# A four-layer transformer kernel: the opening without diagonal matrices, feed-forward subtractions moved, high-half passes sent first

## The reference, cut

```python
x = x + quant_xattn(layernorm(x), fside, ctx)   # int8-style: gate/up product, silu, down product
x = x + bit_ffn(layernorm(x), w1, w2, w3)       # ternary weights, 704 hidden
x = x + xattn(layernorm(x), ctx, mask, Wq, Wk, Wv, Wo)   # 16 heads of 128
x = x + moe_ffn(layernorm(x), router, sh_gate, sh_up, sh_down, r_gate, r_up, r_down)

def smooth_quant_linear(x, w):       # quant_xattn runs it twice
    s = sqrt(max(amax_cols(x), EPS) / max(amax_cols(w), EPS))
    xs, ws = x / s, w * s
    x_scale, w_scale = amax_rows(xs) / 127, amax_rows(ws) / 127
    return round(xs / x_scale) @ round(ws / w_scale).T * x_scale * w_scale.T
```

## Time and profile before

| | us |
| --- | --- |
| median of three runs | 431.57 (431.56 to 433.33) |
| profiled execution | 431.38 |
| its span | 429.3 |
| TensorE busy | 402.8 (94%) |
| VectorE busy | 307.4 (72%) |
| ScalarE busy | 230.3 (54%) |
| GpSimd busy | 175.1 (41%) |

### The profile page before, as it was taken

One profiled execution on the slowest core, in us unless ns is written; L12 is line 12 of the kernel. 1 busy time (PEld: TensorE's weight loads), 2 busy tenths in 40 slices (PEclk: granted clock), 3 DMA queues, 4 the chain that ended last, 5 costly groups with the idle time before them and its releaser, 6 DMA issues.

```text
span 429.3 us, 8839 instructions
## 1 busy us (share of the span) xinstructions
PE 402.8 (94%) x3185; PEld 382.6 (89%) x3185; DVE 307.4 (72%) x948; ACT 230.3 (54%) x636; POOL 175.1 (41%) x294
## 2 busy tenths in 40 slices
PE   7877979999989999999999999999999999999795
PEld 7766868999979999999999999999899999998795
DVE  5599676968865888787766879777757766654544
ACT  2678656665644446666543456656453566564231
POOL 2124665565634352525533354355342233332231
PEclk9999999999999999999999999999999999999899
DMA  7997200000000020000000100000000000000000
GB/s 252 328 352 293 76 2 0 3 2 0 2 2 0 8 71 0 2 2 3 1 14 14 52 2 2 2 1 2 2 26 2 2 0 3 2 2 0 26 0 26
DMA packets 15098, 16.89 MB, mean 39 GB/s; under 512 B 1552, under 2 KB 14032, under 8 KB 15056
## 3 DMA queue, kind: packets, MB, share of 16 engines
q1 hardware_dynamic: 15056, 16.33, 11.8%
HBM read 15.28 MB, written 1.05 MB: 38 GB/s over the span
## 4 chain that ended last, share of the span: by engine, by line
PE 57%; DVE 22%; ACT 10%; issue 5%; POOL 5%; DMA 1%; DVEq 0%; POOLq 0%
PE bank_s L350 13%; PE bank_u L350 9%; PE bank_qa L350 7%; PE bank_o L350 7%; PE bank_pt L533 4%; PE bank_pt L350 4%; DVE prob L1502 3%; ACT prob L838 3%; PE bank_x L350 3%; DVE pt_lo L1513 2%; DVE ut_lo L1519 2%; PE bank_u L462 2%; ACT pt_hi L798 1%; POOL prob L1135 1%; PE bank_x L358 1%
## 5 line engine op out<-in xcount | busy, mean ns | idle before, releaser
L1135 POOL TENSOR_SCALAR prob<-prob,row_inv,valid_b 128x256 f32<-128x256 f32 x128 | 70.3, 558 | 92.6 <-DVE row_inv L1509 92.2
L838 ACT ACTIVATE prob<-prob,row_min 128x256 f32<-128x256 f32 x128 | 64.2, 502 | 68.5 <-DVE row_min L1502 68.3
L1513 DVE TENSOR_TENSOR pt_lo<-bank_pt,pt_hi 128x512 fp32r<-128x512 f32 x64 | 44.1, 688 | 18.1 <-ACT pt_hi L798 17.9
L1519 DVE TENSOR_TENSOR ut_lo<-bank_u,ut_hi 128x256 fp32r<-128x256 f32 x64 | 26.9, 421 | 35.2 <-ACT ut_hi L798 34.5
L1502 DVE CUSTOM_DVE_ANT_0 prob<-bank_s,masked 128x256 f32<-128x256 f32 x128 | 48.8, 418 | 2.9 <-PE bank_s L350 2.4
L1147 POOL TENSOR_TENSOR act_lo<-act_raw,act_hi 128x256 fp32r<-128x256 f32 x32 | 24.2, 755 | 49.2 <-ACT act_hi L903 49.2
L798 ACT ACTIVATE pt_hi<-bank_pt 128x512 fp32r<-128x512 f32 x64 | 37.6, 587 | 9.4 <-PE bank_pt L533 9.2
L350 PE MATMUL bank_o<-c_hi,ut_hi 128*128 128x256 f32 x128 | 38.7, 302 | 1.8 <-DVE ut_lo L1519 1.6
L533 PE MATMUL bank_pt<-ident,prob 128*128 128x128 f32 x256 | 38.9, 274 | 0.8 <-POOL prob L1135 0.7
L350 PE MATMUL bank_qa<-xt_hi,a_hi 128*128 128x256 f32 x126 | 39.5, 314 | 0.0
L350 PE MATMUL bank_u<-pt_hi,cx_hi 128*128 128x256 f32 x128 | 37.7, 295 | 1.6 <-DVE pt_lo L1513 1.4
(11 more groups left out here) (306 smaller groups left out, 1328.7 us busy)
## 6 DMA issues: line engine op xcount, KB each, us to landing
wq_raw<-in_wqT SPq DMA_DIRECT2D x4, 512.0 KB, 9.4
wo_raw<-in_wo SPq DMA_DIRECT2D x4, 512.0 KB, 8.9
w_raw<-in_w12T SPq DMA_DIRECT2D x2, 704.0 KB, 6.8
gate_raw<-in_gateT SPq DMA_DIRECT2D x2, 576.0 KB, 7.6
up_raw<-in_upT SPq DMA_DIRECT2D x2, 576.0 KB, 9.4
down_raw<-in_downT SPq DMA_DIRECT2D x2, 576.0 KB, 11.3
x<-in_x SPq DMA_DIRECT2D x4, 256.0 KB, 5.3
guT<-in_guT SPq DMA_DIRECT2D x4, 256.0 KB, 3.0
```

Of the source, the lines that this page charges most:

```text
L838: last = act.activation(row, row, ACT.Exp, scale=-1.0, bias=row_min[:, h % 2, t:t + 1], accum_out=row_sum[:, h % 2, t:t + 1])
L1135: last = pool.tensor_scalar(row, row, row_inv[:, h % 2, t:t + 1], valid_b[:, 0:1], ALU.mult, ALU.mult)
L1513: dve.tensor_tensor(pt_lo[:, :, :].rearrange("p s t -> p (s t)"), bank["pt"][:, :], f32(pt_hi[:, :, :].rearrange("p s t -> p (s t)")), ALU ...
L1519: dve.tensor_tensor(ut_lo[:, :], bank["u"][:, 0:T], f32(ut_hi[:, :]), ALU.subtract).then_inc(S["u_l"], 1)
```

## The change

The computation stays the same. Five things differ:

1. The diagonals are gone. A scale column, repeated 128 times along the free dimension, is itself the stationary operand and the identity moves (`q_spread`). In the opening the roots are made in two instructions and each is spread on its own; the weights' scales are spread as soon as they are there, before the rounded values are turned, and ScalarE copies them before the product.
2. The opening is ordered anew on all engines: fillers, `prep_unit`s (order 0, 2, 1, 3, other banks), ternary steps; `q_weight_scales(1)` goes from behind the ternary layer to before the second `q_dequant`; `ctx_split_lo(0)` from before the first ternary chunk to behind the second.
3. GpSimd's feed-forward subtractions: none before the ternary chunks now, two after, four after `lna`, one each in the heads 2, 4, 5, 6, 7 and 8.
4. In `bit_down`, `scores`, `mix`, `project` and `ffn_down` the passes with the high half of the newly made operand go first, behind a wait for that half alone; then comes the wait for the low half and its passes. The number of passes is the same.
5. Layer norms signal each tile by itself, and the turn waits tile by tile.

```diff
-FFN_LO_HEADS = (2, 5, 6, 8)
+FFN_HI_HEADS = (2,)
+FFN_HI_EARLY = FFN_UNITS - len(FFN_HI_HEADS)
+FFN_LO_HEADS = (2, 4, 5, 6, 7, 8)
...
+        PREP_ORDER = (0, 2, 1, 3) + tuple(range(4, 2 * PAIRS))
...
+            def turn_xn(b, kind, dst):
+
+                for t in range(NT):
+                    pe.wait_ge(S[kind + "_xn"], NT * b + t + 1)
...
             def q_spread(b, s):
-                pe.wait_ge(S["q_diag"], 2 * b + s + 1)
-                w = 512 if s == 0 else 256
-                dst = bank["x0"] if s == 0 else bank["x1"]
-                pe.matmul(dst[:, 0:w], ones[:, :], dg[:, 0:w // P, :].rearrange("p a c -> p (a c)"),
-                          start=True, stop=True).then_inc(S["q_spread"], 1)
+
+                for i in range(2):
+                    pe.wait_ge(*(S["q_root"], b + 1) if s else (S["q_roots"], q_roots_count(b, i)))
+                    columns = [root0[:, i, b, k:k + 1] for k in range(ND)] if s == 0 else [sis[:, i:i + 1]]
+                    dst, at = spread_place(b, s, i)
+                    for j, column in enumerate(columns):
+                        last = pe.matmul(dst[:, at + j * P:at + (j + 1) * P], column.to_broadcast([P, P]), ident[:, :],
+                                         start=True, stop=True)
+                    last.then_inc(S["q_spread"], 1)
+
+            def q_spread_weight_scales(b, s):
+                pe.wait_ge(S["q_scales"], 2 * b + s + 1)
+                if b > 0 and s == 0:
+                    pe.wait_ge(S["q_bf_w"], b + 1)
+                if b == 0 and s == 1:
+                    pe.wait_ge(S["prep_lo"], 4)
+                for j in (2, 3):
+                    last = pe.matmul(wscale_bank(b)[:, (j - 2) * P:(j - 1) * P],
+                                     qscale[:, s, j:j + 1].to_broadcast([P, P]), ident[:, :], start=True, stop=True)
+                last.then_inc(S["q_wspread"], 1)
 
...
-                pe.wait_ge(S["q_wdiag"], 2 * b + s + 1)
-                pe.matmul(bank["x1"][:, 0:D], ones[:, :], dg[:, 2:4, :].rearrange("p a c -> p (a c)"),
-                          start=True, stop=True).then_inc(S["q_prod"], 1)
+                last.then_inc(S["q_prod"], 1)
...
             def bit_down(b, c):
                 if c == 0:
                     pe.wait_ge(S["w3_ready"], 2)
+                    pe.wait_ge(S["prep_lo"], 8)
                 pe.wait_ge(S["bit_hi"], BIT_CHUNKS * b + c + 1)
...
-                        keep_busy(*((5, "s1"), (10, "pt"))[c - BIT_CHUNKS])
+                        keep_busy(*((3, "s1"), (4, "pt"))[c - BIT_CHUNKS])
...
             def mix(b, h):
 
-                pe.wait_ge(S["t_l"], H * b + h + 1)
+                pe.wait_ge(S["t_h"], H * b + h + 1)
                 if h >= 1:
                     pe.wait_ge(S["u_l"], H * b + h)
+                elif b > 0:
+                    pe.wait_ge(S["shared_x"], b)
                 for s in range(2):
-                    last = split_mm(bank["u"][:, 0:T], cx_hi[:, s, :], cx_lo[:, s, :], pt_hi[:, s, :],
-                                    pt_lo[:, s, :], s == 0, s == 1)
+                    for half in (cx_hi, cx_lo):
+                        pe.matmul(bank["u"][:, 0:T], half[:, s, :], pt_hi[:, s, :], start=(s == 0 and half is cx_hi),
+                                  stop=False, skip_group_check=True)
+                pe.wait_ge(S["t_l"], H * b + h + 1)
+                for s in range(2):
+                    last = pe.matmul(bank["u"][:, 0:T], cx_hi[:, s, :], pt_lo[:, s, :], start=False, stop=(s == 1),
+                                     skip_group_check=True)
                 last.then_inc(S["u_mm"], 1)
 
             def project(b, h):
...
             keep_busy(22, "pt")
             q_turn_xn(0)
-            keep_busy(24, "pt")
+            keep_busy(16, "pt")
             q_piece(0, 0)
-            keep_busy(30, "pt")
+            keep_busy(28, "pt")
+            q_spread_weight_scales(0, 0)
+            keep_busy(8, "pt")
             q_piece(1, 0)
             pe.wait_ge(S["abs_done"], 6)
             pe.matmul(bank["u"][:, 0:6], ones[:, :], gsum[:, :], start=True, stop=True).then_inc(S["gamma_mm"], 1)
             q_piece(2, 0)
             prep_unit(0)
             prep_unit(1)
+            q_piece(3, 0)
             prep_unit(2)
-            q_piece(3, 0)
             prep_unit(3)
-            keep_busy(16, "pt")
+            keep_busy(8, "pt")
             q_piece(4, 0)
+            keep_busy(18, "pt")
+            q_spread_weight_scales(0, 1)
+            keep_busy(5, "pt")
+            q_piece(5, 0)
             prep_unit(4)
+            q_piece(6, 0)
             prep_unit(5)
             prep_unit(6)
-            q_piece(5, 0)
-            q_piece(6, 0)
             prep_unit(7)
             keep_busy(24, "pt")
             bit_turn(0)
             keep_busy(6, "pt")
             pe.wait_ge(S["w12_ready"], 4)
-            pe.wait_ge(S["prep_lo"], 8)
+            pe.wait_ge(S["prep_lo"], 4)
+            pe.wait_ge(S["q_wscale"], 2)
 
             def beside_bit(c):
                 if c == 1:
@@ -812,8 +875,8 @@
...
-            def q_spread_diagonals(b, s):
...
-            def q_scale_diagonals(b, s):
-
-                pool.wait_ge(S["q_scales"], 2 * b + s + 1)
-                pool.nop(nofuse=True)
-                for j in (2, 3):
-                    last = pool.tensor_scalar(dg[:, j, :], ident[:, :], qscale[:, s, j:j + 1], 1.0, ALU.mult, ALU.mult)
-                last.then_inc(S["q_wdiag"], 1)
...
+            q_roots0()
             q_round(0, 0, 0)
-            q_scale_diagonals(0, 0)
             q_root1(0)
             q_round(0, 1, 0)
-            q_scale_diagonals(0, 1)
             power(0, "lnb")
-            pool.wait_ge(S["lnb_xn"], 1)
-            lnq_power(1, 2)
+            for c in range(BIT_CHUNKS):
+                bit_low(0, c)
+                if c == 1:
+                    lnq_power(1, 2)
             ffn_weights_lo(0)
             ffn_weights_lo(1)
-            for c in range(BIT_CHUNKS):
-                bit_low(0, c)
-            ffn_weights_lo(2)
-            ffn_weights_lo(3)
             power(0, "lna")
-            pool.wait_ge(S["lna_xn"], 1)
-            for u in range(4, FFN_LO_EARLY):
+            pool.wait_ge(S["lna_xn"], NT)
+            for u in range(2, FFN_LO_EARLY):
                 ffn_weights_lo(u)
             normalise(0, 0)
             q_roots(1)
-            q_spread_diagonals(1, 0)
             for b in range(NB - 1):
                 batch(b, False)
...
-            q_spread_diagonals0(0)
...
             ternary12_clip(1, 0)
-            prep_lo(4)
             ternary12_clip(1, 1)
-            ternary3_clip(0)
-            prep_lo(5)
-            prep_lo(6)
+            q_weight_scales(1)
             q_dequant(0, 1).then_inc(S["q_out"], 1)
             q_residual0()
             ln_stats_of(0, "lnb")
+            prep_lo(4)
+            ternary3_clip(0)
+            ln_apply(0, "lnb")
+            prep_lo(5)
             ternary3_clip(1)
-            prep_lo(7)
-            ln_apply(0, "lnb")
             dve.wait_ge(S["x_in"], 16)
             link(lnq_stats_of([1]))
+            ln_lo(0, "lnb", xt_hi, xt_lo)
+            prep_lo(6)
             lnq_variances([1])
-            ln_lo(0, "lnb", xt_hi, xt_lo)
-            ctx_split_lo(0)
             for c in range(BIT_CHUNKS):
                 bit_act(0, c)
                 if c == 0:
-                    mask_row(0)
+                    prep_lo(7)
+                elif c == 1:
+                    ctx_split_lo(0)
                 elif c == 2:
                     prep_lo(8)
                 elif c == 3:
+                    mask_row(0)
+                    dve.wait_ge(S["router_hi"], 1)
+                    dve.tensor_tensor(router_lo[:, :, :], router_raw[:, :, :], f32(router_hi[:, :, :]), ALU.subtract
+                                      ).then_inc(S["router_lo"], 1)
+                elif c == 5:
                     lnq_apply(1)
-            q_weight_scales(1)
             prep_lo(9)
             bit_residual(0)
             ln_stats_of(0, "lna")
@@ -1801,9 +1831,6 @@
             first_queries_lo(1)
             row_minima(0, 0)
             row_minima(0, 1)
-            dve.wait_ge(S["router_hi"], 1)
```

214 lines of the change are left out of this document (108 added, 106 removed).

## The result

| | before | changed |
| --- | --- | --- |
| median, us | 432.45 (431.56 to 434.01, 4 runs) | 419.16 (418.34 to 419.98, 4 runs) |
| profiled execution, us | 431.38 | 418.34 |
| its span | 429.3 | 416.5 |
| mean granted clock in it | 0.996 | 1.000 |

The ratio is 0.9689, with a 95% interval of 0.9649 to 0.9729: 3.1% faster. The forecast was 419.5 us (416 to 424), faster. One execution of a later experiment, low waits back, took 1352.38 us and is the only one counted as slow: it is left out of every comparison of spans, and moves that experiment's median by 0.02 us.

The account below looks back on a forecast made before the run. Time can be won only where TensorE stands still, in the opening and at passages between layers. The profiled 431.4 less 7.3 (opening) and 5.0 (body) gives 419.1, as median 419.3, called 419.5 us with unseen hops; range 416 to 424.

Parts of the forecast that it names:

- The opening: The chain through all engines up to the turn of `lna`, forecast to come 7.3 us earlier.
- second dequantisation: In the opening, at 32.75 us before: another 1.2 us saved here, 3.9 us in all.
- Spread and copy ahead of the product: At the second dequantisation: 0.9 of 1.24 us goes, 0.2 comes back in fillers.
- The two diagonals: Ahead of the second dequantisation: half of 0.87 us and a handover go, 0.5 us.
- The opening keeps half its gain: Rival, 15%: one late ternary step holds the opening's chain, 3.6 us less gain, 423 us.
- Two `gate_lo` beside the layer norm, +0.2: Behind `bit_residual`: the layer norm's small `TENSOR_SCALAR` ends with the two `gate_lo`, at about 49.8, costing 0.2 us.
- The rival with more collisions in the heads: Rival, 5%: GpSimd's six subtractions in the heads bring two more collisions of 1.4 us with VectorE, 422.3 us.
- The body: Behind the turn of `lna`: shorter waits for low halves and normalised rows, -5.0 us (-2.5 to -6).
- Turns by tiles: In the body, at the last turn and two others: turning tile by tile saves 0.6 us.
- The clock: Rival, 15%: the fall at 402 to 406 us, left in place, goes (10%, 417.8) or one more comes (5%, 421.2).
- One more fall, in the shorter opening: Rival, 5%: another fall of the clock in the opening with its fillers moved, 421.2 us.
- Slower: Rival, 3%: satisfied waits in the midst of TensorE's groups cost 45 ns (gain gone) or 120 ns (20 us slower, 440).

Follow-up runs that it names:

- low waits back: The changed kernel with only the waits for the low halves moved back ahead of the high passes; 426.40 us, ratio to before 0.9848.
- Stall back: The changed kernel with `q_weight_scales(1)` alone put back behind the ternary layer of batch 0; 423.30 us, ratio to before 0.9774.
- High halves first: The kernel before with only the high passes put first in five functions, the low half's wait behind them; 427.82 us, ratio to before 0.9873.
- tiles back: The changed kernel with only the tile-wise waits undone, so turns wait for both tiles; 420.56 us, ratio to before 0.9730.
- opening alone: The changed kernel with low halves' waits ahead of the high passes again and turns waiting for both tiles; 426.30 us, ratio to before 0.9875.
- more waits: The changed kernel with 492 more already satisfied waits in TensorE's order, in `mix`, `project` and `ffn_down`; 420.52 us, ratio to before 0.9715.

## Why the prediction was right

**What bounds it.** Time could be won only where TensorE stands still: the heads are 3.29 us apart as before, and the gain stands in the opening and at the passages.

**The opening, -7.3 forecast, -6.45 measured.** The chain's steps were right, and the stall's cause too. The estimates of its first half were each a little high: the spread from the roots took 1.6 us off instead of 2.0. The step that was mis-sized is *second dequantisation*: 1.2 us more than at the first were to be won, 0.6 came. Its two terms came out differently. Spread and copy ahead of the product, with the fillers, were to give 0.7 and gave 0.85 (second scaling to dequantisation, 6.07 us before, 5.22 now). The two diagonals were to give 0.5 and gave nothing: the second scaling, at 26.68 before, is at 24.62, 2.1 us earlier where the first dequantisation had been 2.3 (timelines, before and changed):

```profile
26.68 0.47 DVE L1382 TENSOR_TENSOR qw<-cx,bank_x 128x128 f32<-128x128 f32 x2
```

```profile
24.01 0.69 DVE L1738 SCALAR_TENSOR_TENSOR c_lo<-bank_s,c_hi 128x512 fp32r<-128x512 f32 x1 [0.22 <-ACT c_hi L861]
24.62 0.47 DVE L1404 TENSOR_TENSOR qw<-cx,bank_x 128x128 f32<-128x128 f32 x2
```

ScalarE takes the tanh at 19.34, behind `prep_hi(0)`, TensorE's two `wo` units stand ahead of the spread, and VectorE's `c_lo` of the second unit ahead of the scaling. "The opening keeps half its gain" described that kind of loss, not its amount. That the chain then lay near the landing of `wo_raw` was in no sentence of the forecast; the wait is up to 2.1 us long, and one of 1.3 us moved the turn of `lna` by 1.25. From `xt_lo` on the forecast held: 4.25 us more were to be won up to the turn of `lna` (7.3 less 3.05), and 4.5 came. "Two `gate_lo` beside the layer norm, +0.2" did not come: the small `TENSOR_SCALAR` (`ln_ve`) is at 50.65, when the two have all but ended, and takes 0.17 us; `bit_residual` to the turn is 3.4 us against 3.7, and these 0.3 are the tiles.

**The port.** Stall back shows the row again, 2.72 us to the end of `gate_lo`. The Trainium skill, page SBUF — State Buffer, section Who interferes with whom, has it that a VectorE instruction in a two-port mode and a GpSimd one exclude each other for a whole instruction. The trace agrees as far as that goes; here VectorE stood through two GpSimd instructions one behind the other (2.76 us for both). By the same rule `x<-bank_u,x`, with one of its inputs in PSUM, is free beside `gate_lo`, and so it was (0.69 at 48.72). The rival with more collisions in the heads did not come: six subtractions or four there differ by 0.3 us at most.

**The body, -5.0 forecast, -4.65 measured besides the clock.** High halves first was to give 2.7 + 0.7 + 0.5 + 0.3 + 0.35 = 4.55; alone it gave 4.9 at like clock, and 5.3 when it was taken out of the changed kernel. By batches, from the turn of `lna` on to the next: 1.3 us at the end of attention of batch 0, 0.3 at that of batches 1 and 2, 1.45 in batch 3. Turns by tiles were to give 0.6 in the body; with the opening's 0.2 and 0.3 that is 1.1, and 1.3 was measured, 0.95 of it in the body. From the turn of `lna` to the last turn, the low waits back cost 4.6 us, the tiles back 0.95 and both together (opening alone) 5.4, where the changed kernel is only 4.5 shorter than before: the difference is the 0.9 that stays unexplained.

**The clock.** The forecast left the fall of the earlier trace rows in place and gave 10% to its going. In the profiled execution it went, 1.7 us, and covered the opening's shortfall of 0.85 and the body's of 0.35. So the number 419.5 is better than its terms, and that is luck: without it, the profiled execution would have been about 420.0 (418.34 + 1.7), and the two executions of the changed kernel that had one fall took 419.53 and 419.98. "One more fall, in the shorter opening" (5%) was underrated: two of the ten profiled executions with this opening have one from 22 to 26 us, behind the wait for `wo_raw`. The falls were taken for a property of one place; they differ from one execution to the next. TensorE: Matmul & The Clock Gate of the Trainium skill, section Part 1: The HAM clock gate, has it for the rise at a kernel's start that its instant varies from run to run. Here it is the number of falls that varies, 0.984 to 0.996 of mean clock in the kernel before.

**Slower, by 272 waits.** Out: 492 more cost nothing. The rival's own sum was off besides: 272 waits of 120 ns are 32.6 us, so 20 us slower than before would have been about 452 us, not 440.

## What to carry to other kernels

Where an operand comes in two halves, put the wait for the late one directly ahead of the first pass that uses it: the satisfied waits added here cost under 1 ns each, and the passes before the wait cover the making of the late half. On a critical chain keep small VectorE instructions like `amax<-amax`, which reads and writes SBUF, away from long GpSimd ones, but check that the place they go to is not on the chain as well. When an opening has been shortened, look up what lands by transfer next: an instruction in TensorE's order that waits for a weight holds everything behind it, and what other engines make from it as well.

## What was not expected of the hardware

The mean granted clock of one and the same kernel ran from 0.984 to 0.996 before (428.6 to 432.3 us of span), from 0.995 to 1.000 in the four executions of the changed kernel, and from 0.987 to 1.000 in the six of more waits, so the median of a few executions can move by more than the change is worth: 2.2 us of stall at full clock became 4.1 in the median, and 1.6 us saved in the kernel before, at like clock, became nothing. The landing of `wo_raw` varied from one profiled execution to the next: the first unit that needs it began at 20.90 us without a wait in the changed kernel, and at 22.36 behind a wait in opening alone, 1.5 us apart at least. No execution with the order of before shows more than 0.2 us of it.
